# Gated linear attention on one Trainium2 core: keys' products and scans of two rows of values in one Vector instruction each

## The reference, cut to what matters

```
q = (x @ Wq).reshape(b, t, h, dk) * scale
k = (x @ Wk).reshape(b, t, h, dk)
v = (x @ Wv).reshape(b, t, h, dv)
gk = jax.nn.log_sigmoid(x @ Wgk1 @ Wgk2 + bgk2) / GATE_LOGIT_NORMALIZER
def step(S, inp):
    qt, kt, vt, gt = inp
    S = S * jnp.exp(gt)[..., None] + kt[..., None] * vt[..., None, :]
    ot = jnp.einsum('bhk,bhkv->bhv', qt, S)
    return (S, ot)
S0 = jnp.zeros((b, h, dk, dv), x.dtype)
...
o = o * jax.lax.rsqrt(jnp.mean(o * o, axis=-1, keepdims=True) + EPS) * norm_w
o = o * (g * jax.nn.sigmoid(g))
return o.reshape(b, t, vd) @ Wo
```

## Time and profile before

| | |
|---|---|
| median of 3 runs | 2053.62 us (2052.46 to 2054.06) |
| the profiled execution | 2058.37 us, of it 2056.6 us span |
| TensorE matmul busy | 1910.5 us (93%) |
| VectorE busy | 1080.4 us (53%) |
| ScalarE busy | 808.6 us (39%) |
| GpSimd busy | 520.7 us (25%) |
| mean granted TensorE clock | 0.981 of full speed |
| the stage of the change | 1352.7 to 1528.3 us of the span |

### The profile page before, as it was taken

The page is one execution under the profiler, slowest core; times in us unless marked ns, Lnnn a source line. Parts: engine busy times, 40 slices in busy tenths (PEclk is TensorE's granted clock), DMA queues, the critical chain, the costliest instruction groups (busy, mean ns, idle before and its releaser), DMA issues. The chain is left out here.

```text
span 2056.6 us, 30390 instructions
## 1 busy us (share of the span) xinstructions
PE 1910.5 (93%) x11502; PEld 1255.6 (61%) x11502; DVE 1080.4 (53%) x2430; ACT 808.6 (39%) x1780; POOL 520.7 (25%) x623
## 2 busy tenths in 40 slices
PE   6999989999999999999999999989987798999876
PEld 5556656666666776677667766733354555556643
DVE  4766676757523234333333332378874665556444
ACT  2553544545443323432343233234423234445332
POOL 2332332223201111101010110045642243552222
PEclk9999999999999999999999999999999999999998
DMA  6000000000020000000000000020000000000001
GB/s 238 1 1 1 1 1 1 1 1 1 1 79 1 1 1 1 1 1 1 1 1 1 1 1 1 1 74 1 0 1 1 1 1 1 2 1 2 1 1 41
DMA packets 9776, 24.03 MB, mean 12 GB/s; under 512 B 2449, under 2 KB 6305, under 8 KB 8865
## 3 DMA queue, kind: packets, MB, share of 16 engines
q1 hardware_dynamic: 8336, 18.92, 2.5%
q10 hardware_dynamic: 1296, 3.18, 0.4%
HBM read 20.00 MB, written 2.10 MB: 11 GB/s over the span
## 5 line engine op out<-in xcount | busy, mean ns | idle before, releaser
L1586 PEld LDWEIGHTS ps<-cos_vx,cos_probs 128*128 128x128 f32 x2048 | 238.7, 191 | 31.4 <-issue 30.1
L1586 PE MATMUL ps<-cos_vx,cos_probs 128*128 128x129 f32 x2048 | 239.1, 274 | 1.0 <-DVE cos_on L1209 1.0
L1577 PE MATMUL ps<-lead_room,cos_kT 128*128 128x512 f32 x512 | 230.7, 594 | 4.0 <-ACT lead_room L1429 2.4
L1458 ACT ACTIVATE cos_probs<-ps 128x512 f32<-128x512 f32 x256 | 150.6, 597 | 165.0 <-PE ps L1577 163.8
L690 ACT ACTIVATE probs<-sc,nmax 128x512 f32<-128x512 f32 (+3 forms) x256 | 132.6, 524 | 188.2 <-DVE nmax L544 188.2
L1358 POOL TENSOR_TENSOR cos_qrs<-cos_qse,neg_half 128x4 f32<-128x4 f32 x59 | 59.5, 1008 | 443.7 <-DVE cos_qse L1191 443.7
L1577 PEld LDWEIGHTS ps<-lead_room,cos_kT 128*128 128x128 f32 x512 | 94.5, 190 | 104.7 <-issue 98.5
L1189 DVE TENSOR_REDUCE cos_qss<-cos_qsq 128x4 f32<-128x512 f32 x59 | 40.5, 686 | 223.7 <-ACT cos_qsq L1437 223.7
L799 PE MATMUL sc<-kT,qT 128*128 128x512 f32 (+3 forms) x512 | 149.4, 435 | 5.2 <-DVE probsT L556 2.5
L3092 DVE TENSOR_REDUCE cos_wq<-ps 128x2 f32<-128x1024 f32 (+3 forms) x128 | 101.8, 822 | 69.0 <-PE ps L3305 60.2
L799 PEld LDWEIGHTS sc<-kT,qT 128*128 128x128 f32 x512 | 85.4, 190 | 71.5 <-issue 53.4
(11 more groups left out here) (508 smaller groups left out, 3403.5 us busy)
## 6 DMA issues: line engine op xcount, KB each, us to landing
onT<-in_mla_wqT SPq DMA_DIRECT2D x1, 2048.0 KB, 9.5
lead_room<-in_mla_wo SPq DMA_DIRECT2D x1, 2048.0 KB, 19.8
cos_wq<-in_cos_wq SPq DMA_DIRECT2D x1, 2048.0 KB, 25.6
cos_wout<-in_cos_wout SPq DMA_DIRECT2D x1, 2048.0 KB, 7.5
out<-x SPq DMA_DIRECT2D x4, 512.0 KB, 2.9
x<-in_x SPq DMA_DIRECT2D x1, 1536.0 KB, 15.0
wq_pe<-in_mla_wq_pe ACTq DMA_DIRECT2D x1, 1024.0 KB, 14.6
x<-in_x SPq DMA_DIRECT2D x1, 512.0 KB, 4.2
```

What stands on the lines that cost most here:

```text
L1458: act.activation(probs[:, n % 2, kj, :], ps[:, kj, :], ACT.Exp).then_inc(s["e_done"], 1)
L1577: pe.matmul(ps[:, kj, :], kT[:, b % 2, kj * P:(kj + 1) * P], qT[:, hq % 2, h % 4, :], start=True, stop=True).then_inc(s["s_ready"], 1)
L1586: last = pe.matmul(po[:, qi // 2, qi % 2, :], probs[:, n % 2, kj, qi * P:(qi + 1) * P], vx[:, b % 2, kj, :], start=(kj == 0), stop=(kj == ...
```

## The change

The two products of a step become one instruction of 1024 columns over both banks, with the keys read twice. The two scans become one of 1024 columns. So that the state starts from 0 again at the second row, the decays of a batch are laid out twice, one copy behind the other, with a 0 in the first column of each copy. ScalarE therefore makes two exponentials of 511 columns instead of one of 512. The zeros are set once, at the start of the stage (for both sets, two columns each). The second set of decays moves to a part of `lead_room` that nothing else uses in this stage. The scan now raises `st_ready` by 2 at its end, and waits once for `qs_ready` of step t - 2, for the value the second scan waited for.

```diff
@@ cosine attention, scalar engine, last batch, h == 13
-                                act.activation(rec["decay"][:, 0, :], z, ACT.Exp, scale=1.0 / GATE_NORMALIZER)
+                                for w in range(2):
+                                    act.activation(rec["decay"][:, w, 1:], z[:, 1:], ACT.Exp, scale=1.0 / GATE_NORMALIZER)
@@ gated_linear_attention
+        decays = (decay[:, :, :].rearrange("p n s -> p (n s)"), room[:, 10 * S:12 * S])
@@ scan(t)
-                    for w in range(2):
-                        dve.tensor_tensor(ps[:, pair[w], :], ps[:, pair[w], :], kT[:, b % 2, :], ALU.mult)
+                    both = ps[:, pair[0]:pair[1] + 1, :]
+                    series = both.rearrange("p w s -> p (w s)")
+                    dve.tensor_tensor(both, both, kT[:, b % 2, :].unsqueeze(1).to_broadcast([P, 2, S]), ALU.mult)
                     dve.drain()
                     if p == 0 and b > 0:
                         dve.wait_ge(s["decay_ready"], b)
-                    for w in range(2):
-                        if t >= 2:
-                            dve.wait_ge(s["qs_ready"], 2 * (t - 2) + w + 1)
-                        dve.tensor_tensor_scan(st[:, t % 2, w, :], decay[:, b % 2, :], ps[:, pair[w], :], 0.0,
-                                               ALU.mult, ALU.add).then_inc(s["st_ready"], 1)
+                    if t >= 2:
+                        dve.wait_ge(s["qs_ready"], 2 * (t - 1))
+                    dve.tensor_tensor_scan(st[:, t % 2, :, :].rearrange("p w s -> p (w s)"), decays[b % 2], series, 0.0,
+                                           ALU.mult, ALU.add).then_inc(s["st_ready"], 2)
@@ vector engine, start of the stage
                 dve.memset(eps[:, :], GLA_EPS)
+                for d in decays:
+                    for w in range(2):
+                        dve.memset(d[:, w * S:w * S + 1], 0.0)
+                dve.drain()
@@ scalar engine
-                def decays(b):
+                def make_decays(b):
                     act.wait_ge(s["lg_ready"], b)
-                    act.activation(decay[:, b % 2, :], z[:, :], ACT.Exp,
-                                   scale=-1.0 / GATE_NORMALIZER).then_inc(s["decay_ready"], 1)
+                    for w in range(2):
+                        last = act.activation(decays[b % 2][:, w * S + 1:(w + 1) * S], z[:, 1:], ACT.Exp,
+                                              scale=-1.0 / GATE_NORMALIZER)
+                    last.then_inc(s["decay_ready"], 1)
```

More of the change, by code:

```diff
@@ L2088, in project @@
                         copy(("v", b, 1), vT[:, b % 2, 1, :])
-                        decays(b)
+                        make_decays(b)
                 act.wait_ge(s["setup"], 1)
```

## The result

The changed kernel takes 2059.49 us, the median of 13 runs (2056.91 to 2062.81). The kernel before took 2053.62 us over the 13 runs beside them (2047.57 to 2058.75). The ratio is 1.0034, with a 95% interval of 1.0026 to 1.0043: slower. The medians lie 5.9 us apart, and the ratio makes it about 7 us. The time lies in my range of 2050 to 2060, but near its end, and the change is a loss that can be told, where I had called it none.

What follows compares the result with a forecast made beforehand. VectorE was taken to bound plain steps and TensorE 65.7 us of gapless stretches. Terms 3.2 + 0.5 - 0.8 gave +2.9 us, added to the median: 2056.5 us; own range 2054 to 2058.5, 8-in-10 range 2050 to 2060.

Steps and rivals of the forecast that it cites:

- point 8: TensorE's clock behind 1427.48: the idle gap shrinks to about 2 us; staying at 2.4 GHz gives -1.6, half taken, -0.8 us.
- Points 1 and 2: Start: memsets and a drain, +0.3 us; to the scan of step 4: four steps -0.5, collisions +1.8, balance +1.5.
- Point 3: Sums of step 4 wait for GpSimd, 1.07 us later: first full TensorE stretch begins and ends at +2.6 us.
- Point 4: Steps 10 to 14, VectorE's: steps -0.6, `finish_ffn` +0.9, log decays -0.4, wait for TensorE +0.1 us; balance stays +2.6.
- Point 5: From the output piece at 1427.48 to 1485, TensorE's queue sets the time apart from one gap; balance stays +2.6 us.
- Point 6: Steps 25 to 30: VectorE gains 0.7 us, but step 31's product comes +0.6 instead of -0.7; balance +3.2.
- Point 7: Tail, VectorE's statistics: L76 stands behind GpSimd's later gating product, 0 to +1.0 us, 0.5 taken.
- rival C: Slower by TensorE's clock: two more 5 us stretches fall to 1.2 GHz, +6.9 us, 2060.5 us; 0.16 with the scan's cost.
- The saving per step: VectorE's queue becomes 0.12 us shorter per step from the merged product and scan, 3.8 us over 32 steps.
- points 1 to 7: The path from the stage's start through its tail, without TensorE's clock: 3.2 + 0.5 us.
- Rival A: No stretch anchored to GpSimd, no collision bites: VectorE's saving comes through outside the 65.7 us, -2.1, 2051.5 us; chance 0.24.
- B: Each instruction's fixed part is saved whole, 0.15 us for 64 instructions, less delays: about -6, 2047.5 us; chance 0.04.

## Why the prediction was right or wrong

The direction of the sum was right, its size was not: +2.9 us forecast, +7.8 in the stage and 6 to 7 in the runs. The step that failed is point 8, TensorE's clock: a term of -0.8 us that measured some +4 in the traces. The trace after allows a check of each point, in us after the stage's first memset, after minus before.

- **Points 1 and 2 held.** The first product came 0.27 us later (forecast 0.3), the scan of step 4 at 22.93 instead of 21.47, +1.46 (+1.5). Its parts were not quite right: collisions 0.7 and 0.8 us instead of 0.8 and 1.0, and four steps saved 0.3 instead of 0.5. (The terms of point 2 and the +0.3 of point 1 add up to 1.6 and not to the 1.5 that was carried on; it changes nothing here.)
- **Point 3 held for the start and failed for the length.** The sums of step 4 came +2.54 late (+2.6). But the stretch they opened then ran at 1.2 GHz, and the product of step 10 came +5.5 late instead of +2.6. Between the two lie 28.10 us after the change and 25.13 before, and 25.12 or 25.13 in the four other runs read for this whose clock was high there (late GpSimd with and without fillers, fillers, GpSimd held). In the trace after, the scan of step 10 is this one:

```profile
1405.15 2.29 DVE L1853 TENSOR_TENSOR_SCAN gla_st<-lead_room,ps 128x1024 f32<-128x1024 f32 x1
```

- **Point 4, 0 forecast, measured +1.4.** `finish_ffn` took 0.83 us more (0.9), the log decays 0.27 less (0.4). The rest is the clock again, in the pieces from 1410 on, so that the product of step 13 waited 0.92 us instead of 0.1.
- **Point 5 held.** From the addition at +6.95 to the product of step 25 at +6.93 nothing changed on balance.
- **Point 6 failed by 0.6.** The scan of step 31 came at +6.90. Part of the output piece ran at full clock this time (3.14 us), and VectorE waited 0.38 us instead of more than 0.73.
- **Point 7: +0.9, the top of its range.** L76 ran beside GpSimd's gating product (1514.22 to 1515.49) and took 1.29 us instead of 0.17.
- **Point 8 was the mis-sized term.** I gave the clock -0.8. TensorE waited 2.41 us before the output piece at 1430.82 instead of 3.11, as forecast, but ran at 1.2 GHz all the same (3.67 us), so this place gave back nothing. And two stretches that had been at full clock fell. By the fillers, the clock holds 8.2 us of the changed kernel's stage and 4.2 of that of the kernel before: +4 instead of -0.8. The runs' ratios give 6.4 and 3.9 us for the same, +2.5, with 95% intervals of 2 to 3 us to either side of each. That is the mechanism of my rival C, to which I gave 0.16 together with the scan's cost; it decided at the sums of step 4, one of the places that wait for GpSimd, and again at step 10.
- **The saving per step** was 0.04 us, not 0.12. The scan took 2.287 us (2.27) and the product 1.223 (1.22). But from product to scan it was 1.34 us in a plain step, as with two products before (1376.48 to 1377.82), so the shorter product saved nothing there; it came to 1.29 when the wait was moved.

With fillers on both sides the long scan and what comes with it cost 175.38 less 171.64, 3.7 us: about the sum of points 1 to 7 (3.2 + 0.5). The two have different sets of fillers, set where each trace had its slow stretches, so this is a comparison of the two at a high clock (0.98 and 0.99) and not of one edit. So the sum of the path came out and the clock on it did not. That 3.7 holds the gain of the merged product too: the long scan alone costs 6.6 us of the stage with fillers (175.38 less 168.80) and 10.1 without. Rival A is out (the first stretch was anchored to GpSimd), and so is B: the direction is against both. What is not shown is how regular the slow stretches are. The run with the wait first and that with GpSimd held had fewer or shorter ones in the first stretch, all have some, and one profile stands for each kernel. The two groups of times of late GpSimd alone, 2052 to 2057 and 2062 to 2064 us, speak for stretches that are slow in some executions and not in others; no trace of the second group shows it.

Of the two rules of the Trainium skill that the prediction cites, the exclusion between GpSimd and VectorE ("SBUF — State Buffer", who interferes with whom) was tried both ways on L76 and L1877 (0.85 and 3.25 us beside GpSimd, 0.17 and 1.38 with it held back); for L1895 and L1897 (1.04 and 1.16 us, before 0.89 and 0.16) only the lengths agree. The fixed cost that a large tile pays once ("VectorE: DVE Perf Modes", the section on the errata) has little to give here: a merged product is 0.06 us shorter than the pair, where each of a pair ran 0.15 longer than its columns.

## What to carry over

Merging two instructions saves only what a pair shows beyond one of double length, here 0.05 of 1.2 us. It costs the early start of whoever reads the first half, here 1.07 us in every step. So merge what has a reader that waits for both anyway (the products, -2.8 us), and leave apart what hands over in halves (the scans, +10 us of the stage). And where one engine's queue waits for another before long work, a longer wait may cost twice, since TensorE may come back at half its clock: small fillers in the waits took 8 us off the changed kernel's stage. They do not replace the early start: with them the long scan still cost 6.6 of its 10 us, and the kernel before gained 4 us from its own.

## What the runs showed that I had not expected

A wait that has long been fulfilled, between a drain and a scan of 1024 columns, took 0.06 us (a plain step of 3.55 us became one of 3.49 when it was moved away). With the scan of 512 columns behind the same merged product and such a wait in the same place, product and scan were 1.28 us apart. Why the long scan alone pays for it stays open.

Behind a wait of TensorE of 1.50 us between repeats and sums the clock was found at 1.2 GHz (1377.05), where the kernel before with waits of about 0.4 us stayed at 2.4 GHz. With 16 small bf16 products in that wait the clock there stayed high. But a wait of 1.56 us at 1493.47 of the same trace had the full clock behind it, so the length of the wait does not decide alone, and what else does stays open here.
